# Six local-attention layers: the inverse norms taken by GpSimd, in a clamp and a power, instead of by a chain of eleven VectorE instructions

## The reference

```python
def l2norm(t):
    return t / jnp.maximum(jnp.linalg.norm(t, axis=-1, keepdims=True), 1e-12)

def attn_layer(x, Wqkv, qs, ksc, Wo):
    q, k, v = jnp.split(x @ Wqkv, 3, -1)          # 16 heads of 64, window 32
    q = l2norm(q) * qs
    k = l2norm(k) * ksc
    ...                                           # rotary turn of q and k
    out = local_attention(q, k, v)
    return out @ Wo

def ffn_layer(x, g, bln, W1, b1, W2, b2):
    mu = x.mean(-1, keepdims=True)
    var = ((x - mu) ** 2).mean(-1, keepdims=True)
    xn = (x - mu) / jnp.sqrt(var + 1e-05) * g + bln
    a, gate = jnp.split(xn @ W1 + b1, 2, -1)
    return a * jax.nn.gelu(gate, approximate=False) @ W2 + b2
```

## Time and profile before

| | us |
|---|---|
| three runs | 4378.6, 4396.46, 4422.52 |
| median | 4396.46 |
| the profiled execution | 4409.03, span of its instructions 4407.3 |
| part B (from its first tile's norms to the last), about | 1017 to 4320 |

### The profile page before, as it was taken

How to read it: one execution, slowest core, us unless ns; L and a number is a source line. 1 busy time by engine, 2 the same in 40 slices (tenths; PEclk the granted TensorE clock), 3 DMA queues, 4 the chain that set the end, 5 groups by cost and what they waited for, 6 DMA issues and landing times. The chain is left out here.

```text
span 4407.3 us, 153325 instructions
## 1 busy us (share of the span) xinstructions
PE 3998.6 (91%) x66018; PEld 2914.3 (66%) x66018; DVE 3520.4 (80%) x5436; ACT 2544.9 (58%) x4654; POOL 2552.0 (58%) x1429
## 2 busy tenths in 40 slices
PE   7899999986998999999999999999999999999996
PEld 4555555545776777777776777777776777777774
DVE  5655555536888889999988898999988889998993
ACT  4544555534555666656656566666665566666563
POOL 2333333326666676667666666667766666666662
PEclk7866666658999999999999999999999999999997
DMA  1000000001211122221211122122121111212112
GB/s 46 4 3 2 2 2 2 3 26 41 54 49 48 48 54 55 53 56 48 62 54 47 49 54 54 52 56 56 48 54 52 51 54 49 56 50 53 50 48 61
DMA packets 122834, 188.19 MB, mean 43 GB/s; under 512 B 24910, under 2 KB 44134, under 8 KB 121964
## 3 DMA queue, kind: packets, MB, share of 16 engines
q1 hardware_dynamic: 122220, 179.07, 15.0%
HBM read 23.78 MB, written 4.19 MB: 6 GB/s over the span
## 5 line engine op out<-in xcount | busy, mean ns | idle before, releaser
L1251 POOL TENSOR_TENSOR rc<-rc,rnorm 128x1024 f32<-128x1024 f32 x384 | 734.5, 1933 | 358.5 <-DVE rnorm L205 358.5
L1245 POOL TENSOR_TENSOR rc<-rc,rs 128x1024 f32<-128x1024 f32 x384 | 905.2, 2369 | 34.5 <-DVE rs L1313 30.8
L1273 POOL TENSOR_TENSOR prob_b<-prob_b,rinv 128x1024 f32<-128x1024 f32 x192 | 365.9, 1906 | 653.0 <-DVE rinv L1386 653.0
L562 POOL TENSOR_TENSOR prob<-prob,rden 128x512 f32<-128x512 f32 (+3 forms) x128 | 297.6, 2325 | 661.3 <-DVE rden L674 661.3
L1307 DVE TENSOR_TENSOR rc<-proj,rope_b 128x1024 f32<-128x1024 f32 x384 | 469.2, 1222 | 114.9 <-PE proj L853 63.8
L941 PE MATMUL ring<-pT,vmoved 64*64 64x32 f32 x18432 | 436.0, 221 | 115.1 <-issue 113.8
L1093 ACT ACTIVATE oT_b<-ring 128x512 f32<-128x512 f32 x384 | 209.6, 596 | 564.6 <-PE ring L941 564.6
L941 PEld LDWEIGHTS ring<-pT,vmoved 64*64 64x64 f32 x18432 | 401.0, 135 | 179.5 <-issue 162.3
L890 PEld LDWEIGHTS ring<-ident,rc 128*128 128x128 f32 x3072 | 362.3, 143 | 235.5 <-POOL rc L1251 77.2
L890 PE MATMUL ring<-ident,rc 128*128 128x128 f32 x3072 | 455.9, 278 | 62.2 <-POOL rc L1251 59.4
L1321 DVE TENSOR_REDUCE sums<-squares 128x16 f32<-128x1024 f32 x384 | 460.2, 1198 | 44.5 <-ACT squares L1105 42.3
(11 more groups left out here) (163 smaller groups left out, 8837.0 us busy)
## 6 DMA issues: line engine op xcount, KB each, us to landing
vmoved<-vown SPq DMA_DIRECT2D x576, 128.0 KB, 2.4
vmoved<-vown SPq DMA_DIRECT2D x192, 192.0 KB, 2.5
vmoved<-vown SPq DMA_DIRECT2D x576, 64.0 KB, 2.1
wqkv_raw<-in_L_ffn_Wqkv SPq DMA_DIRECT2D x40, 192.0 KB, 2.7
wo<-in_L_ffn_Wo SPq DMA_DIRECT2D x6, 512.0 KB, 4.2
x_attended<-xtok SPq DMA_DIRECT2D x8, 256.0 KB, 2.0
xtok_c<-x_attended SPq DMA_DIRECT2D x8, 256.0 KB, 4.4
out<-xtok_c SPq DMA_DIRECT2D x8, 256.0 KB, 2.5
```

The source lines that it names most:

```text
L1245: nc.gpsimd.tensor_tensor(rc[:, k % 2, c, :], rc[:, k % 2, c, :], rs[:, c, :], ALU.add).then_inc(add_done, 1)
L1251: nc.gpsimd.tensor_tensor(dst, dst, rnorm[:, k % 2, c * HEADS:(c + 1) * HEADS].rearrange("p (h o) -> p h o", o=1).broadcast_to([P, HEADS, ...
L1273: nc.gpsimd.tensor_tensor(pr, pr, rinv[:, :, :].rearrange("p q (s o) -> p q s o", o=1).broadcast_to([P, PAIRS, 2, KEYS]), ALU.mult).then_i ...
```

## The change

VectorE's `norms_of` goes. GpSimd gets `inverse_norms(k, m)` at the end of its step: a clamp (TENSOR_SCALAR, maximum with 1e-24) from `sums` into `rnorm`, a wait for it, and a TENSOR_TENSOR that raises `rnorm` to the power in a new tile `minus_half`, filled with -0.5. VectorE keeps the reading of the variances (`read_variance`) and the widening copy (`widen_deviation`), which now waits for GpSimd and stands at the start of the next step. `rn_done` counts one per tile.

```diff
-        rtmp = sb("rtmp", [P, 2 * HEADS + TILES])
+        minus_half = sb("minus_half", [P, 2 * HEADS + TILES])
...
+            nc.gpsimd.memset(minus_half[:, :], -0.5).then_inc(zeroed, 1)
...
+            def inverse_norms(k, m):
+
+                lo = 0 if tile(k) else 2 * HEADS
+                hi = 2 * HEADS + (TILES if m is not None else 0)
+                if tile(k):
+                    pool.wait_ge(ss_done, 2 * k + 2)
+                if m is not None:
+                    pool.wait_ge(var_read, m + 1)
+                    need(pool, spread_done, m)
+                nc.gpsimd.tensor_scalar(rnorm[:, k % 2, lo:hi], sums[:, lo:hi], 1e-24, None, ALU.max).then_inc(clamp_done, 1)
+                pool.wait_ge(clamp_done, min(k, NT) + 1)
+                nc.gpsimd.tensor_tensor(rnorm[:, k % 2, lo:hi], rnorm[:, k % 2, lo:hi], minus_half[:, lo:hi], ALU.pow).then_inc(rn_done, 1)
+
             def scale_heads(c, k):
-                pool.wait_ge(rn_done, (k + 1) * RSQRT_STEPS)
+                pool.wait_ge(rn_done, k + 1)
...
                 if tile(g + 1):
                     add_halves(1, g + 1)
+                if tile(g + 1) or seq_at(g, 6) is not None:
+                    inverse_norms(g + 1, seq_at(g, 6))
...
-            def norms_of(k, m):
...
-                    nc.vector.tensor_scalar(ss, ss, 1e-24, None, ALU.max).then_inc(clamp_done, 1)
...
-                rsqrt(nc, dve, sums[:, lo:hi], rnorm[:, k % 2, lo:hi], rtmp[:, lo:hi], rn_done, i * RSQRT_STEPS)
...
+            def read_variance(m, k):
+                dve.wait_ge(var_full, m + 1)
+                need(dve, rn_done, min(k, NT))
+                nc.vector.tensor_scalar(sums[:, 2 * HEADS:], proj_bank(0, 1)[:, 0:TILES], 1e-5, None, ALU.add).then_inc(var_read, 1)
+
+            def widen_deviation(k):
+                dve.wait_ge(rn_done, min(k, NT) + 1)
+                nc.vector.tensor_copy(dev, rnorm[:, k % 2, 2 * HEADS:].rearrange("p (t o) -> p t o", o=1)
+                                      .broadcast_to([P, TILES, P])).then_inc(spread_done, 1)
...
             for g in STEPS:
                 up, rest = seq_at(g, 7), seq_at(g, 8)
+                if up is not None:
+                    widen_deviation(g)
...
-                if tile(g + 1) or seq_at(g, 6) is not None:
-                    norms_of(g + 1, seq_at(g, 6))
+                if seq_at(g, 6) is not None:
+                    read_variance(seq_at(g, 6), g + 1)
```

More of the change, by code:

```diff
@@ L835, in _ @@
         def _(pe):
-            pe.wait_ge(zeroed, 6)
+            pe.wait_ge(zeroed, 7)
             def begin(name, k):
@@ L1075, in _ @@
         def _(act):
-            act.wait_ge(zeroed, 6)
+            act.wait_ge(zeroed, 7)
             def stage_hi(n, half):
@@ L1292, in _ @@
         def _(dve):
-            dve.wait_ge(zeroed, 6)
+            dve.wait_ge(zeroed, 7)
             dve.wait_ge(consts_in, 16)
@@ L1319, in square_sums @@
                 if c == 0:
-                    need(dve, rn_done, k * RSQRT_STEPS)
+                    need(dve, rn_done, k)
                 nc.vector.tensor_reduce(sums[:, c * HEADS:(c + 1) * HEADS],
@@ L1323, in square_sums @@
                                         AX.X, ALU.add).then_inc(ss_done, 1)
-            def norms_of(k, m):
[L1327 to L1332, removed]
-                    nc.vector.tensor_scalar(ss, ss, 1e-24, None, ALU.max).then_inc(clamp_done, 1)
[L1334 to L1340, removed]
-                rsqrt(nc, dve, sums[:, lo:hi], rnorm[:, k % 2, lo:hi], rtmp[:, lo:hi], rn_done, i * RSQRT_STEPS)
-                if m is not None:
-                    nc.vector.tensor_copy(dev, rnorm[:, k % 2, 2 * HEADS:].rearrange("p (t o) -> p t o", o=1)
-                                          .broadcast_to([P, TILES, P])).then_inc(spread_done, 1)
+            def read_variance(m, k):
[6 more added lines that the diff above has]
+                                      .broadcast_to([P, TILES, P])).then_inc(spread_done, 1)
             def add_attention(n, half):
```

## The result

The changed kernel takes 5162.9 us (median of four, 5156.3 to 5181.5); the kernel before takes 4409.5 us beside it. The ratio is 1.173, 95% interval 1.165 to 1.181. The forecast was 4330 us, with a range of 4280 to 4800; the time lies 363 us above the range. The profiled execution of after has a span of 5166.4 us.

What follows compares the result with a forecast made beforehand. TensorE and VectorE stood at nine tenths busy, the norms on the path in one or two steps of four. Gains of 16 + 14 + 17 + 18 = 65 us off 4396 gave 4331, say 4330; range 4280 to 4800.

Steps and rivals of the forecast that it cites:

- The power, X: Length of GpSimd's power between add_halves and scale_heads: taken as 1.1 us, range 0.25 to 4.9.
- the prediction's own table: By kind of step, 48 each: loss of 48 us per us of X beyond that kind's slack, less 35 us.
- Rival 2: GpSimd's path to scale_heads becomes the bound, slower: X = 3 gives 4556, X = 4.9 gives 4920; chance 0.32.
- from 1.43 on, another 48 from 1.69, 2.1 and 2.7 on: X in us where tiles 60, 58, 57 and 59 begin to lose; first two from existing waits, others from slack.
- the 35 us taken off: Gains credited at any X: 17 us from remaining scale_heads waits and 18 us from ScalarE's emptying of banks.
- Clamp and hand-overs: Added on GpSimd after add_halves: clamp 0.25 us, each hand-over 0.11 to 0.12 us, together 0.5 us besides the power.
- The widening copy ... No cost: VectorE's copy, 0.43 us, now behind GpSimd's power: done at 2045.1, TensorE wants it at 2045.69, so no cost.
- The rest of the 77.2 us ... taken in full: TensorE's remaining waits for scale_heads, after 46 and 14 us for two kinds of tile: 17 us gained.
- a fifth, 18 us: Share of TensorE's 92 us of waits for ScalarE's late emptying of banks taken as gain; bounds zero and 55.
- Rival 3: GpSimd's scale_heads starts first and holds VectorE's copy for 3.77 us in one step of four: 4512; chance 0.05.
- Rival 1: Power of 1.5 to 2.3 us: old VectorE and new GpSimd paths cancel, no change, 4403 at X = 2; chance 0.22.
- Rival 4: VectorE is the real bound, so all TensorE idle time goes, 215 us in part B: 4180; chance 0.03.

Runs made afterwards that it cites:

- p8: Changed kernel with GpSimd's power taken over the last 8 columns only (most heads not normalized): 4399.7 us, +3 against the kernel before.
- p16: Changed kernel with the power taken over the last 16 columns only (half the columns not normalized): 4547.7 us, +151 against the kernel before.
- split: Changed kernel with q's 16 columns clamped and powered between the two add_halves, q's scale_heads waiting for that power alone: 5120.2 us.
- warm2: Changed kernel with filler products on TensorE where it waits (14, 6, 14, 0 by kind of tile, 12 ahead of spread): 4989.3 us.
- p0: Changed kernel with one cheap instruction, a rough first guess, in place of the power (norms rough): 4373.9 us, -22 against before; repeated, 4386.3.
- varfirst: Changed kernel with the variance's 4 columns powered first, with their own semaphore for VectorE's widening copy: 5121.3 us.
- both: Changed kernel with q's power between the two add_halves and the variance's 4 columns powered first under their own semaphore: 4966.2 us.

## Why the prediction was wrong, point by point

- **The power, X.** This is the step that failed first: "14 passes at GpSimd's 2.13 ns for 32 columns and one fixed part are ... 1.1 us". It measured 5.46 us, and 6.16 in one kind of step. The passes of a plain product say nothing of a power: 2.0 ns a column for the one, 158.5 for the other. The upper bound failed too. "Five times the passes are 4.9 us" was a multiple of my own guess, no row bounded it, and the range stopped at X = 4.3. In the prediction's own table this one term turns a gain of 65 us into a loss of 667, and its sign of being wrong, a power over 2.3 us, came true. I had weighed two rules of the Trainium skill (GPSIMD Engine Reference, "Performance versus the Vector engine" and "Performance pitfalls for Q7 kernels"); the estimates from them, 0.3 and 1.7 us, were both below the trace's 5.46.
- **Rival 2, GpSimd's path becomes the bound.** This happened (chance 0.32). "Each us of X costs 48 us from 1.43 on, another 48 from 1.69, 2.1 and 2.7 on" was right in kind, and for 1.43 and 1.69 also in size: the waits of these two kinds are within 0.2 us of it at X = 2.93 and 5.46. The 2.1 and 2.7 were too early: at 2.93 those waits had grown by 0.16 and 0.00 us and not by 0.83 and 0.23. That +147 met +151 there is in part luck, since the 35 us taken off were not there either. At the true X the table gives +667 of the 753. That it begins to cost somewhere between 1.7 and 2.9 us is shown by `p8` and `p16`.
- **Clamp and hand-overs.** "Together 0.5 us": clamp 0.29, then 0.08 and 0.07 us, so 0.44. Right.
- **"The widening copy ... No cost".** Wrong at this X: VectorE waited 203.5 us for the power ahead of it, and TensorE 129.7 us for the copy, 3.22 us at the `spread` shown. I priced the copy by the time TensorE wants it, with X = 1.1, and did not carry X on into it in rival 2. Taking the copy off the long power gave 56 us alone, and 133 on top of `split`.
- **The clock.** No term of the sum had it. `warm2` gives 167 us for it. The earlier trace rows had 0.99, and a rival that lets TensorE wait up to 5 us in a step should have asked what that does to the products behind the wait.
- **"The rest of the 77.2 us ... taken in full" and ScalarE "a fifth, 18 us".** The wait for `scale_heads` could be cut by 56 us, not 77, and ScalarE's waits rose by 45 where I had them fall by 18. Sooner transposes ask for banks sooner. So even X = 0.22 us gains 17 to 22 us, under the 44 that can be told from no change; with X = 1.1, as I took it, there would have been no gain to measure (an estimate, between `p0` and the +3 us of `p8` at 1.67).
- **The other rivals.** Rival 3, the copy loses the port, did not happen in after: the copy took 0.43 us each of 48 times, and the pair at 2260.73 took 4.00 us. It did happen in `p0` (29 of 48 copies took over 1 us, 8 of 48 in its repeat) and in `split` (47 of 48), but for the pair's first instruction only, 2.12 us, and not for the 3.77 of the pair. Rival 1 described X between 1.5 and 2.3, and `p8` shows that case: +3 us. Rival 4, VectorE as the real bound, is out by `p0`: VectorE fell from 453 to 359 of 500 us there, and of TensorE's 32.6 idle us 26.5 stayed.

```profile
2500.00:3000.00 500.00, 473.54 (x9289) 364.20 (x9287) 358.74 (x362) 317.07 (x500) 359.39 (x257) 0.99 0.20 53
```

## What to carry to other kernels

Before work moves to another engine, the duration of the very instruction on that engine has to be measured, alone, at two sizes; a price built from other operations of that engine missed by a factor of five here, and a range built on such a price missed as well. In a table of slacks read from one period's timelines, the terms that rest on a wait that is already there held within 0.2 us up to a dose of 5.5; those that rest on slack came too early, and gains credited to other waits did not come. Compare such a table kind by kind with the trace, not only by its sum. When a wait in the table gets longer than it was anywhere in the trace, follow two more things: who else waits for the same event, and TensorE's clock behind the wait. And idle time in front of an instruction is no free place: it moves when what is ahead of it moves.

## What the runs showed of the hardware

- GpSimd's power costs 0.40 us and 158.5 ns for each column, whether on 32, 64 or 128 partitions: 1.64 us for 8 columns, 5.42 for 32, 10.54 for 64.
- TensorE's granted clock was 0.57 from T1 to the end of a projection behind a wait, 4.93 us for what takes 2.91. Filler products in the waits kept it at 0.99 and made the whole program 167 us shorter, though they add work.
- The port between VectorE and GpSimd showed where I had not looked for it. Copy and scale pair are released by the same power. In after the copy starts 0.04 us ahead of the pair and takes 0.43 us, 48 times of 48. In `split` the pair starts 0.06 us ahead (2517.77 and 2517.83); the copy then took 2.12 us, that is until the pair's first instruction had ended, 47 times of 48. The Trainium skill (SBUF — State Buffer, "Who interferes with whom") has the two exclude each other for a whole instruction, the one that comes first keeping the port, and the trace agrees. In `p0` the copy mostly starts 0.00 to 0.03 us behind the pair, and both happen. All 48 copies (minimum/median/maximum ns) of `p0` and of `split`:

```profile
L1350 DVE COPY hid<-rnorm x48: 416/1158/2170, 1102.5 to 4318.6; 128x512 f32<-128x512 f32 x48
```

```profile
L1355 DVE COPY hid<-rnorm x48: 427/2119/2123, 1167.4 to 5085.2; 128x512 f32<-128x512 f32 x48
```

So some hundredths of a microsecond decide it as long as one event releases both. In `varfirst` and `both`, where the copy has a semaphore of its own, no copy took more than 0.45 us.
